# Cross-attention and mixture of experts on one core: attention slots in another order, keys' stack written right behind the queries'

## The reference

```python
x = x + xattn(layernorm(x), ctx, ctx, mask)   # 16 heads of 16, softmax over 1024 keys, Wq Wk Wv Wo
x = x + ffn(layernorm(x))                     # below
ys = geglu(xf @ Ws1 + bs1) @ Ws2 + bs2        # shared expert, 512 wide
logits = (xf @ Wr + br) / 1.5                 # 12 experts, the best 2, softmax over the two
h = einsum('nd,edh->enh', xf, We1) + be1      # each expert 768 wide, geglu, @ We2 + be2
yr = einsum('end,ne->nd', yE, w)
```

## Time and profile before

| | us |
|---|---|
| three runs | 1130.43, 1139.40, 1134.62 |
| median | 1134.62 |
| profiled execution, its own time | 1124.97 |
| its span (first to last instruction) | 1123.4 |

### The profile page before, as it was taken

How to read it: one execution, slowest core, us unless ns; L and a number is a source line. 1 busy time by engine, 2 the same in 40 slices (tenths; PEclk the granted TensorE clock), 3 DMA queues, 4 the chain that set the end, 5 groups by cost and what they waited for, 6 DMA issues and landing times.

```text
span 1123.4 us, 26481 instructions
## 1 busy us (share of the span) xinstructions
PE 958.6 (85%) x7515; PEld 695.4 (62%) x7515; DVE 717.8 (64%) x1840; ACT 572.8 (51%) x1276; POOL 369.8 (33%) x537
## 2 busy tenths in 40 slices
PE   5578889889888887974699879989998999999896
PEld 3233344444443433853588768878897888788785
DVE  5765768767657745542578567666755677567654
ACT  3136555555545465321264356656655566557553
POOL 5300120444342453127100043533423444343342
PEclk9779999999999999987799989999999999999999
DMA  5534316253352132134644463544424445425232
GB/s 150 140 76 107 76 52 151 84 126 93 92 122 87 59 111 80 47 107 150 211 161 143 134 187 71 134 104 95 103 43 124 90 93 133 124 44 136 32 56 43
DMA packets 107918, 117.19 MB, mean 104 GB/s; under 512 B 20396, under 2 KB 99960, under 8 KB 107648
## 3 DMA queue, kind: packets, MB, share of 16 engines
q1 hardware_dynamic: 87168, 67.97, 21.9%
q0 software_dynamic: 20064, 47.20, 17.2%
q10 hardware_dynamic: 560, 0.53, 0.2%
HBM read 73.91 MB, written 38.87 MB: 100 GB/s over the span
## 4 chain that ended last, share of the span: by engine, by line
PE 41%; issue 4%; DVE 3%; DMA 2%; another core or an unknown queue 2%; ACT 1%; DVEq 0%; SPq 0%; ACTq 0%; POOL 0%; POOLq 0%
PE ff_psH L2218 27%; PE ff_psY L2233 13%; PE ff_psX L2203 1%; DVE ff_actf L2442 1%; DMA ff_xrow<-expert_in 1%; DMA expert_in<-ff_zeros 1%; DVE ff_actl L2435 1%; DVE xl L2425 0%; ACT xh L2284 0%; ACT ff_gel L2298 0%; DMA out_dram<-ff_x 0%; DMA ff_x<-out_dram 0%; ACT ff_acth L2293 0%; POOL out_dram L2188 0%
## 5 line engine op out<-in xcount | busy, mean ns | idle before, releaser
L2218 PE MATMUL ff_psH<-xh,ff_wx 128*128 128x256 f16 (+1 forms) x1872 | 292.3, 266 | 29.0 <-issue 15.6
L2218 PE MATMUL ff_psH<-xl,ff_wx 128*128 128x256 f16 (+1 forms) x936 | 241.1, 266 | 1.2 <-issue 1.2
L1122 DVE TENSOR_REDUCE fast_negm<-fast_psS 128x2 f32<-128x512 f32 x256 | 169.1, 686 | 100.1 <-PE fast_psS L513 90.5
L2218 PEld LDWEIGHTS ff_psH<-xh,ff_wx 128*128 128x128 f16 x1872 | 179.2, 100 | 53.0 <-issue 29.3
L2188 POOL DMA_INDIRECT out_dram<-ff_ysc,ff_trow x78 | 124.7, 1599 | 213.9 <-ACT ff_ysc L2340 198.6
L884 ACT ACTIVATE fast_PT<-fast_psT 128x512 f32<-128x512 f32 x256 | 145.6, 597 | 78.5 <-PE fast_psT L545 74.3
L2442 DVE SCALAR_TENSOR_TENSOR ff_actf<-ff_psH,ff_b1T,ff_gel 128x256 f32<-128x256 f32 (+1 forms) x234 | 105.9, 454 | 113.3 <-ACT ff_gel L2298 107.5
L2298 ACT ACTIVATE ff_gel<-ff_psH,ff_b1T 128x256 f32<-128x256 f32 (+1 forms) x234 | 105.5, 452 | 98.4 <-PE ff_psH L2218 85.6
L2233 PE MATMUL ff_psY<-ff_wx,ff_acth 128*128 128x256 f16 x840 | 139.9, 273 | 0.0
L2293 ACT ACTIVATE ff_acth<-ff_actf 128x256 f16<-128x256 f32 (+1 forms) x282 | 110.4, 391 | 32.6 <-DVE ff_actf L2442 31.2
L513 PE MATMUL fast_psS<-fast_Kz,fast_Qs 128*128 128x512 f16 x256 | 100.3, 402 | 30.1 <-DVE fast_negm L1122 22.3
(11 more groups left out here) (266 smaller groups left out, 1631.2 us busy)
## 6 DMA issues: line engine op xcount, KB each, us to landing
ff_st<-in_L_ffn_We_dram POOLq DMA_DIRECT2D x12, 1536.0 KB
ff_xrow<-expert_in SPq DMA_DIRECT2D x41, 256.0 KB, 2.8
ff_st<-in_L_ffn_We_dram POOLq DMA_DIRECT2D x12, 768.0 KB
fast_Qs<-qstk SPq DMA_DIRECT2D x48, 128.0 KB
fast_xbuf<-in_x_dram SPq DMA_DIRECT2D x8, 512.0 KB, 5.4
fast_words<-in_mask_BxSxS_bk_dram SPq DMA_DIRECT2D x8, 512.0 KB, 3.9
fast_xres<-in_x_dram SPq DMA_DIRECT2D x8, 512.0 KB, 4.2
out_dram<-fast_x1s SPq DMA_DIRECT2D x8, 512.0 KB, 5.2
```

The source lines that it names most:

```text
L1122: nc.vector.tensor_reduce(negm[:, two(b), t, 2 * p:2 * p + 2], src, AX.X, ALU.max, negate=True).then_inc(sem["max_done"], 1)
L2218: mm = nc.tensor.matmul(psH[j % stage.banks][:, (half + 1) * NB - rows:(half + 1) * NB], a[:, dt, lo:lo + P], x[:, dt, NB - rows:], start= ...
```

## The change

On SyncE the slot's order changes. The stack of the queries, the write of the keys and the stack of the keys come right behind the write of the queries; the loads of x and of the context stand behind them, and the mask words of batch b are loaded in slot b behind its maxima, not in slot b - 1.

```diff
 def slot(b):                       # SyncE
     if real(b):
         max_rows(b)
+        if b > 0:
+            load_words(b)
...
     if real(b + 2):
         write_q(b + 2)
+    if real(b + 2):
+        stack_q(b + 2)
+        write_k(b + 2, 0)
+        stack_k(b + 2, 0)
     if real(b + 4):
         load_x(b + 4)
     if real(b + 3):
         load_ctx(b + 3, 0)
-    if real(b + 2):
-        stack_q(b + 2)
-    if real(b + 1):
-        load_words(b + 1)
-    if real(b + 2):
-        write_k(b + 2, 0)
-        stack_k(b + 2, 0)
```

```diff
-MISC = dict(oX1=2, mT=0, xT0=0, xT1=1, Q0=0, Q1=2, x2T0=1, x2T1=1, oX2=1, R=0, oX3=2, V=1, cT=0, K=0, onT0=2, onT1=2, O0=1,
+MISC = dict(oX1=2, mT=0, xT0=1, xT1=0, Q0=1, Q1=2, x2T0=0, x2T1=0, oX2=1, R=0, oX3=2, V=1, cT=0, K=0, onT0=1, onT1=2, O0=1,
...
-AT_END = {("x2T1", B - 2): 0, ("x2T1", B - 1): 0, ("onT1", B - 1): 0}
+AT_END = {("x2T1", B - 2): 1, ("x2T1", B - 1): 1, ("onT1", B - 1): 0}
...
     def scores(b, n):              # TensorE
+        if n == 0 and not general:
+            stacks_ready(b)
...
             step()
+            weigh(b - 1, 5)
+            step()
             if real(b):
                 m_T(b)
             step()
             if real(b + 2):
                 x_T(b + 2, 0)
-            weigh(b - 1, 5)
-            step()
             rest()
             begin(1)
             if real(b + 2):
                 x_T(b + 2, 1)
+            weigh(b - 1, 6)
+            if real(b + 2):
                 q_proj(b + 2, 0)
-            weigh(b - 1, 6)
             rest()
             begin(2)
             if real(b + 2):
                 q_proj(b + 2, 1)
-            step()
             if real(b - 2):
-                x2_T(b - 2)
+                x2_T(b - 2, [0])
             weigh(b - 1, 7)
-            step()
+            if real(b - 2):
+                x2_T(b - 2, [1])
             if real(b - 1):
                 o_X(b - 1, 2)
...
             begin(5)
             if real(b + 2):
                 k_proj(b + 2, 0)
-            step()
+            if real(b - 1):
+                on_T(b - 1, [0])
+            else:
+                step()
             weigh(b, 2)
             if real(b - 1):
-                on_T(b - 1)
+                on_T(b - 1, [1])
```

```diff
             exp(b - 1, 23, 24)     # ScalarE
+            if real(b - 1):
+                out_T(b - 1, 2)
+            exp(b - 1, 25)
             if real(b):
                 max_T(b)
-            exp(b - 1, 25)
+            exp(b - 1, 26)
             if real(b + 2):
                 set_xT(b + 2, 0)
-            if real(b - 1):
-                out_T(b - 1, 2)
-            exp(b - 1, 26, 27)
+            exp(b - 1, 27)
...
-            exp(b, 16)
+            exp(b, 16, 17)
             if real(b):
                 out_T(b, 1)
-            exp(b, 17, 18, 19)
+            exp(b, 18, 19)
```

```diff
             begin(2)               # VectorE
...
             one_maximum()
             one_maximum()
-            if real(b + 3):
-                ln1_moments(b + 3)
             if real(b + 2):
                 q_low(b + 2, 1)
             rest()
             begin(3)
...
             if real(b + 3):
-                ln1(b + 3)
+                ln1_moments(b + 3)
             rest()
...
             begin(5)
             if real(b + 1):
                 v_bias(b + 1, 0)
-            rest()
-            begin(6)
+            one_maximum()
+            one_maximum()
             if real(b + 2):
                 k_low(b + 2, 0)
+            one_maximum()
+            if real(b + 3):
+                ln1(b + 3)
+            rest()
+            begin(6)
```

More of the change, by code:

```diff
@@ L571, in o_X, with on_T @@
             mm.then_inc(sem["oX_mm"], 1)
-        def on_T(b):
+        def on_T(b, these=range(DT)):
             until(pe, "on_ready", of("on_ready", b, GROUPS))
-            transposes("onT", b, on, "onT_mm", "onT_set")
+            transposes("onT", b, on, "onT_mm", "onT_set", these)
         def o_proj(b, k):
@@ L585, in o_proj, with x2_T @@
             mm.then_inc(sem["o_mm"], 1)
-        def x2_T(b):
+        def x2_T(b, these=range(DT)):
             until(pe, "xn2_ready", of("xn2_ready", b, 1))
-            transposes("x2T", b, xn2_of(b), "x2T_mm", "x2_set")
+            transposes("x2T", b, xn2_of(b), "x2T_mm", "x2_set", these)
         def router(b):
@@ L642, in begin @@
                         across.update(b=b + 1, n=0, end=0)
-                    if k == 1:
-                        stacks_ready(b + 1)
                     across.update(end=sum(SCORES[:k + 1]), share=SCORES[k], turn=0)
@@ L703, in slot @@
             step()
-            weigh(b, 1)
-            step()
             if real(b + 2):
                 c_T(b + 2, 0)
+            step()
+            weigh(b, 1)
             rest()
@@ L792, in first_slot @@
             across.update(b=0, n=0)
-            stacks_ready(0)
             for k in range(1, 8):
@@ L958, in slot @@
             exp(b, 1)
+            if real(b - 1):
+                out_T(b - 1, 3)
             if real(b - 2):
                 set_x2T(b - 2, 1)
-            if real(b - 1):
-                out_T(b - 1, 3)
-            exp(b, 2, 3, 4, 5, 6, 7, 8)
+            exp(b, 2, 3, 4, 5, 6, 7, 8, 9)
+            if real(b + 2):
+                set_cT(b + 2, 0)
+            exp(b, 10)
             if real(b):
                 out_T(b, 0)
-            exp(b, 9)
-            if real(b + 2):
-                set_cT(b + 2, 0)
-            exp(b, 10, 11, 12)
+            exp(b, 11)
+            exp(b, 12)
             if real(b + 2):
@@ L1289, in slot @@
             if real(b + 3):
-                ln1(b + 3)
+                ln1_moments(b + 3)
             rest()
             begin(4)
+            if real(b - 1):
+                normalised_out(b - 1, 3)
             if real(b - 2):
                 logits(b - 2)
-            if real(b - 1):
-                normalised_out(b - 1, 3)
             if real(b - 2):
@@ L1304, in slot @@
                 v_bias(b + 1, 0)
+            one_maximum()
+            one_maximum()
+            if real(b + 2):
+                k_low(b + 2, 0)
+            one_maximum()
+            if real(b + 3):
+                ln1(b + 3)
             rest()
             begin(6)
-            if real(b + 2):
-                k_low(b + 2, 0)
             one_maximum()
```

## The result

| | before | after |
|---|---|---|
| median | 1132.53 us (4 runs, 1129.98 to 1139.40) | 1103.45 us (4 runs, 1100.28 to 1105.07) |
| profiled execution | 1124.97 us, span 1123.4 | 1104.73 us, span 1103.0 |
| ratio, from all runs | | 0.9731, 95% interval 0.9678 to 0.9783 |

A forecast was written before the change was run, and what follows sets the result against it. TensorE was nearest to a bound, idling 50 us in attention slots 0 to 6. Terms summed to 23 us, cut by a third to 16: profiled 1124.97 to 1109, median 1134.62 to 1118.5; range 1104 to 1128, with rivals 1103 to 1136.

The forecast's parts named there:

- The third taken off: Whole sum: waits that go let PE run into the next ones, so 23 us was cut to 16 us.
- A full slot: Slots 1 to 4 of the attention stage: terms sum to a gain of 3.0 us each, 12.0 in all.
- The slot's start: `weigh` 5 ahead of the maxima's transposition and xT0 out of bank 0 remove PE waits: gain 1.2 us a slot.
- Segment 6: Exp 17 ahead of the psV copy, so its score does not wait for a `weigh`: gain 0.8 us a slot.
- segment 5: It gets `k_low` and `ln1`, 2.24 us of DVE work between its five maxima: loss of 0.4 us a slot.
- Segments 2 and 3: `ln1_moments` moves to segment 3: segment 2's 1.27 us wait goes, segment 3's 0.44 becomes 0.85, net 0.9 us.
- SyncE's part: Last key stack can leave some 7 us sooner: slot 1's 1.98 us wait goes, gain 2.0 us once.
- The words: Slot 6: mask words loaded later move POOL's `keep_x1` some 4 us behind `ln2`, gain 1.5 us.
- The slots' ends: Slots 5 to 7, which have no `ln1`: gain taken as 2.0 us each.
- A: Rival, slots 1 to 4: later `ln1` meets POOL's `res_bias`; gain falls to 5 to 10 us, about 1127; chance 0.17.
- B: Rival: ACT is the next bound at each slot's start and in segment 5; about 1129 us; chance 0.16.
- C: Rival: POOL's chain through the scatters passes the slot's end and delays `rstd2`; 14 us slower, 1148; chance 0.08.

The follow-up runs named there:

- before2: The kernel before, unedited, profiled in a session without "remote" stalls: 1094.23 us.
- after2: The changed kernel, unedited, in the same session as `before2`: 1070.01 us, ratio to before 0.9770.
- b_peact: The kernel before with only the new order of TensorE and ScalarE and the banks: 1121.65 us, ratio to before 0.9900.
- loads_next: The changed kernel with the loads of x and context moved to the next slot's start, behind the mask words: 1066.67 us, ratio to before 0.9758.
- best: `loads_next` plus batch 5's first onT transposition in bank 0 and the last slot's keep_x1 behind ln2: 1066.09 us, ratio to before 0.9735.
- words_late: The changed kernel with the mask words loaded behind the context at the slot's end: 1074.45 us, ratio to before 0.9812.
- after3: The changed kernel, unedited, as base of the session of `words_late` and `best`: 1068.26 us, ratio to before 0.9751.
- the third group's session: Session without stalls that ran `before2`, `after2`, `no_sp` and `loads_next`; the kernel before took 1094.96 us in it.
- no_sp: The changed kernel with SyncE's order of before, the wait for the stacks kept at the first score: 1108.03 us, ratio to before 1.0119.

## Why the prediction was wrong in size

**The third taken off.** This step put the size wrong. The sum stood at 23 us, and I went down to 16 for waits that would come back. The gain is 25 to 28. Some waits did come back (0.85 in segment 3, as forecast; 0.15 and 0.28 at the slot's start), but these were in the terms already. Between the profiles of `before2` and `after2` the gain is 22.5 us, the sum almost exactly, but with some luck: slots 1 to 4 gave 16.2 where the terms had 14.0 with the stack, slot 0 gave 2.0 for 1.5, slots 5 and 6 gave 6.9, and 2.6 were lost elsewhere.

**A full slot: idle time right, price wrong.** The terms gave 3.0 us. PE's idle rows add up to 5.5 us a slot in `before2` (slots 2 and 3, 21 rows) and 2.5 in `after2` (12 rows): 3.0 exactly, and that is luck too, for the terms were off and made up for each other. The slot's start gave some 1.8 us (1.2 forecast) and the small waits that the split transpositions cover 1.1 (0.5). Segment 6 gave 0.4 (0.8; the 1.79 us of rows 3 is 0.40 in `before2`), segment 5 lost 0.8 in two waits for maxima (0.4), and 0.3 went near the slot's end. Segments 2 and 3 gave the 0.9 of the forecast. Yet these slots are 4.5 us shorter. The rest is in PE's "busy" time, 43.0 and 41.6 us for the same 248 matmuls at the same clock. How it gets there can be read at the maxima's transposition, `before2` above and `after2` below:

```profile
195.97 0.38 PE L545 MATMUL fast_psT<-fast_Qs,fast_Kz 128*128 128x512 f16 x1
197.17 0.60 PE L535 MATMUL fast_psM<-ident,fast_negm 128*16 128x128 f32 x4 [0.82 <-DVE fast_xres L1150]
```
```profile
188.36 0.39 PE L546 MATMUL fast_psT<-fast_Qs,fast_Kz 128*128 128x512 f16 x1
188.59 0.60 PE L536 MATMUL fast_psM<-ident,fast_negm 128*16 128x128 f32 x4
```

Without a wait the second starts 0.23 us behind the first, though that lasts 0.39; with it, 1.20 us. The wait shown as 0.82 costs 0.97, and so with nearly every stop of these slots: the overlap of two matmuls, some 0.16 us, is lost too. Where I set each step between two neighbouring rows against the shortest such step in the same traces, the losses come to some 7.4 us a slot in `before2` and 3.0 in `after2`, which is nearly the whole 4.5 (an estimate: it hangs on which steps are taken as alike); without them either slot would take some 41 us. Four or five stops fewer a slot make about half of what the idle rows leave out; the rest are slower steps right behind stops (0.1 to 0.26 us each), which carry no idle time in the trace at all.

**SyncE's part.** "Slot 1's 1.98 us goes, and in other slots the stack is merely safer. Gain 2.0 once." In the mechanism this is the step that failed worst. I had read the stack's end 0.1 us ahead of the next slot's first wait and the 1.98 us in slot 1, and not asked what happens when PE's slot gets 4 us shorter while the chain of POOL and SP does not. In `b_peact` it is PE's next wait in slots 1 to 3 (3.28, 2.26 and 1.78 us):

```profile
105.24 1.09 PE L459 MATMUL fast_psM<-ident,fast_xn 128*128 128x128 f32 x4 [3.28 <-DMA fast_Kz<-kmask_rows]
...
199.10 0.63 PE L459 MATMUL fast_psM<-ident,fast_xn 128*128 128x128 f32 x4 [1.78 <-DMA fast_Kz<-kmask_rows]
```

So the part is worth 6 us alone, 38 beside VectorE's and the others'. The total came out near my sum only because each of the other terms had silently assumed that the stack is in time. It is just so: in `after2` the last stack DMA leaves 3.5, 3.3 and 1.3 us ahead of the copies of the maxima that open slots 3, 4 and 5, and the first score of slots 4 and 5, which waits for the stacks, stands 0.43 and 1.33 us ("issue"). In `loads_next` and `best`, whose loads stand elsewhere, it does not.

**The words.** "1.5 us", for the meeting of `ln2` and `keep_x1` in slot 6. `ln2` fell to 1.37 us in slots 5 to 7 as forecast; the whole edit is worth 6 us (`words_late` against `after3`), because with short slots the words also delay the maxima's rows. The forecast named that meeting in slot 6 alone. Before has it in slots 5, 7 and 8 as well (2.61, 3.16 and 3.01 us), and the one in slot 8, the last, the change leaves in place (3.02). The rule that I had quoted from the Trainium skill (SBUF — State Buffer, section on its two separate sides), that one of VectorE and GpSimd can hold a shared port pair for a whole instruction while the other waits, agrees with `best`: the order of the two engines alone takes `ln2` from 3.02 to 1.38 us.

**The slots' ends.** Slots 5 to 7 at 2.0 each: measured in the third group's session 2.9, 4.0, and nothing in slot 7, where a new wait for the maxima's rows stands (0.94 us in `after2`, and in the first profile of the kernel after):

```profile
382.62 0.39 PE L546 MATMUL fast_psT<-fast_Qs,fast_Kz 128*128 128x512 f16 x1 [1.42 <-DMA fast_Qs<-max_rows]
```

Slot 0 at 1.5: 2.0. Slot 1 at 5.0 (3.0 and the stack): 3.0 there, 3.9 in the first profile.

**The rivals.** A, the meeting of `ln1` with `res_bias`, did not happen, but by a hair: in slot 3 POOL's additions ended at 217.79 us and `ln1` began at 218.15. B, ScalarE as the next bound, did not either: PE's waits for it at the slot's start are 0.15 and 0.28 us. The other waits of a full slot in `after2` (0.85, 0.35, 0.42 and 0.25 or 0.60) are all for VectorE's maxima. C, a chain that passes the end of the slot, had the right kind of mechanism in the wrong branch: POOL's scatters were through 5.8 us before the next `rstd2` (231.55 and 237.33 in slot 3), 2.4 us in `after2`, where no stall delays VectorE; the branch over SP's queue passed the end in every version with VectorE's new order and a load in front of the key stack. I had given this 0.08 and judged it by one branch only.

## What to carry to other kernels

When an engine's slot gets shorter, every chain that was just in time is a bound; list the chains that run through the slot with their ends, and price an edit that shortens one by what it costs if it is missing, in the new slot, not in the old. In a queue with waits the order is a dependency: a load that waits for a late producer holds everything behind it, so what others wait for goes first. And on an engine whose instructions overlap, a stop costs more than the idle time that the trace shows for it: here the lost overlap, and behind a long one a stretch at the lower clock.

## What the runs showed of the hardware

- A stop of TensorE costs about 0.16 us beyond its idle time (1.20 against 0.23 us from start to start, with 0.82 shown as idle; 0.14 to 0.17 at 29 of the 33 stops of slots 2 and 3 in `before2` and `after2`).
- After a stop of 5.25 us in `no_sp` TensorE was granted 0.51 of its clock for 6.9 us, and after one of 2.02 us in the kernel after 0.50 for 3.4 us; in `after2`, whose slots 2 to 6 have no stop over 1.93 us, it stayed at 1.00 in them.
- The kernel before took 1133 us in two sessions and 1094 to 1096 us in four others (medians of 4 to 17 runs). "Remote" stalls of ScalarE and VectorE of 1.5 to 5.8 us appear in the attention stage of all six traces of the slower sessions, mostly beside the scatters, and in none of the 14 traces of the other four. They are not the whole difference: from slot 7 on, before takes 727.0 us in its first trace and 708.0 in `before2`, 19 of the 29 us between the two, and there ScalarE has such stalls of 6.3 to 11.9 us in the slower one. Their cause is not shown.
- Within a session the times go with the mean granted clock: the 17 runs of before in the second such session reach from 1129.07 us at 0.956 to 1136.69 at 0.949. Which of the two sets the other is not shown.
